# A two-layer attention and spectral-filter kernel: value rows stored by two transfers, block weights loaded behind the first rows' values, twiddle tables laid out by chunk and loaded later

## What is computed

```
# layer 0: 7 x 7 neighbourhood attention, 4 heads of 32 channels, zero padding, then an MLP
xn = layernorm(x); q, k, v = split(xn @ w_qkv + b_qkv)
attn = softmax(q*scale . windows7x7(k) + rpb);  x = x + (attn . windows7x7(v)) @ w_proj + b_proj
x = x + gelu(layernorm(x) @ w_fc1 + b_fc1) @ w_fc2 + b_fc2
# layer 1 on tokens t (4, 3136, 128): q * sum(k * v), then a spectral filter
t = t + q(ln(t)) * sum_tokens(k(ln(t)) * v(ln(t)))
t = t + selected filter bank: irfft(rfft(phi) * rfft(ln(t))) for +/- parts, mixed by M_phi_plus, M_phi_minus,
        plus a 3-tap part with M_u; one of four banks is chosen by log_weights + gumbel
```

## Time and profile before

| | before |
|---|---|
| median of 3 runs | 1872.19 us (1871.04 to 1874.68) |
| the profiled execution, own time | 1875.25 us |
| its span | 1873.9 us |
| PE busy | 1772.8 us, 95% of the span |
| DVE, ACT, POOL busy | 1285.0, 1177.9, 623.3 us |
| mean granted PE clock | 0.976 of full |
| moved by DMA | 183.74 MB, mean 98 GB/s |
| chain that ended last | PE 69%, DVE 11%, DMA 6%, SP's queue 5%, issue 4%, ACT 3%, POOL 1% |

### The profile page before, as it was taken

The page is one execution under the profiler, slowest core; times in us unless marked ns, Lnnn a source line. Parts: engine busy times, 40 slices in busy tenths (PEclk is TensorE's granted clock), DMA queues, the critical chain, the costliest instruction groups (busy, mean ns, idle before and its releaser), DMA issues.

```text
span 1873.9 us, 76356 instructions
## 1 busy us (share of the span) xinstructions
PE 1772.8 (95%) x32475; PEld 1392.8 (74%) x32475; DVE 1285.0 (69%) x3723; ACT 1177.9 (63%) x2555; POOL 623.3 (33%) x799
## 2 busy tenths in 40 slices
PE   5799999999999998999999999999999999999998
PEld 2466676666667666776788888888888888876675
DVE  2477678888867766464477777777777777647665
ACT  4688888878877664433677777777777777640000
POOL 5454555555555543030522123333222233100000
PEclk8799999999999998999999999999999999999999
DMA  3332333343233224398421222122212221367772
GB/s 94 98 90 77 96 95 86 86 108 105 74 91 100 76 70 123 110 240 193 128 63 37 66 67 67 50 63 66 55 37 66 67 67 51 91 181 206 206 205 70
DMA packets 272608, 183.74 MB, mean 98 GB/s; under 512 B 46496, under 2 KB 269630, under 8 KB 270476
## 3 DMA queue, kind: packets, MB, share of 16 engines
q1 hardware_dynamic: 269390, 177.29, 36.2%
q0 software_dynamic: 640, 1.16, 0.2%
q10 hardware_dynamic: 2240, 0.40, 0.1%
HBM read 108.26 MB, written 70.63 MB: 95 GB/s over the span
## 4 chain that ended last, share of the span: by engine, by line
PE 69%; DVE 11%; DMA 6%; SPq 5%; issue 4%; ACT 3%; POOL 1%; DVEq 0%; ACTq 0%; POOLq 0%
PE banks L1363 20%; PE banks L1341 11%; PE banks L1344 9%; PE banks L403 5%; DVE zone L604 3%; PE banks L1180 3%; PE banks L397 3%; PE banks L1551 3%; PE banks L362 2%; PE banks L352 2%; SPq L1479 2%; PE banks L1175 2%; PE banks L376 2%; DMA YL<-Yd 2%; PE banks L410 2%
## 5 line engine op out<-in xcount | busy, mean ns | idle before, releaser
L1396 DVE COPY Gm<-banks 128x448 f32<-128x448 f32 x896 | 553.0, 639 | 218.3 <-PE banks L1341 136.8
L1382 ACT ACTIVATE Gm<-banks 128x448 f32<-128x448 f32 x896 | 515.8, 629 | 192.8 <-PE banks L1341 147.0
L1363 PE MATMUL banks<-Gm,U 128*32 128x128 f32 x12544 | 517.5, 275 | 9.0 <-issue 8.3
L1363 PEld LDWEIGHTS banks<-Gm,U 128*32 128x32 f32 x12544 | 340.1, 110 | 52.3 <-issue 51.2
L1344 PE MATMUL banks<-V,zone 118*32 118x224 bf16 x7040 | 293.0, 259 | 0.7 <-issue 0.6
L1420 POOL COPY U<-UL 128x896 f32<-128x896 f32 (+2 forms) x28 | 49.9, 1782 | 547.4 <-PE banks L1363 441.9
L1341 PE MATMUL banks<-V,zone 118*128 118x224 bf16 x1824 | 215.5, 261 | 0.7 <-ACT qT L1191 0.6
L866 POOL TENSOR_TENSOR W<-W,mx 128x280 f32<-128x280 f32 x196 | 130.2, 664 | 242.6 <-DVE mx L653 241.3
L1344 PEld LDWEIGHTS banks<-V,zone 118*32 118x32 bf16 x7040 | 193.5, 96 | 1.5 <-issue 1.0
L1341 PEld LDWEIGHTS banks<-V,zone 118*128 118x128 bf16 x1824 | 157.2, 98 | 47.9 <-issue 39.8
L1551 PE MATMUL banks<-YC,zone 98*98 98x256 f32 x768 | 174.5, 389 | 3.3 <-DVE YC L1623 3.3
(11 more groups left out here) (164 smaller groups left out, 2546.3 us busy)
## 6 DMA issues: line engine op xcount, KB each, us to landing
Yd<-YS SPq DMA_DIRECT2D x112, 224.0 KB, 4.4
W<-Vd SPq DMA_DIRECT2D x392, 49.0 KB
zone<-Yd SPq DMA_DIRECT2D x32, 392.0 KB
YL<-Yd SPq DMA_DIRECT2D x32, 392.0 KB
UL<-Ud SPq DMA_DIRECT2D x27, 448.0 KB, 4.1
zone<-Mbf SPq DMA_DIRECT2D x28, 256.0 KB
Vd<-W SPq DMA_DIRECT2D x112, 56.0 KB
T<-XR SPq DMA_DIRECT2D x28, 224.0 KB, 3.7
```

The costliest lines, as they stand in the source:

```text
L1363: ins = e.matmul(p[32 * x:32 * x + 32, :], self.U7[(2 * P + ch) % 3][:, sl, 8 * (3 - q):8 * (3 - q) + 32], self.Gm[:, par, r:r + 2, :], st ...
L1382: e.activation(dst, src, ACT.Copy).then_inc(S["gm_act"], 1)
L1396: v.tensor_copy(dst, src).then_inc(S["gm_dve"], 1)
```

## The change

Four edits, in the code of SP's queue and in one table:

1. A row's values go to `Vd` by two transfers in place of four. One takes the even image lines of the row (partitions 0 to 55), one the odd ones, each with the position in the line as its outermost extent (56), then the four parts, then 128 channels. The counts that are waited for on `d_vs0` and `d_vs1` go from 64 to 32 a row.
2. The six weight loads leave `setup(0)` and become `setup(3)`, at unit 11: behind the stores of rows 0 and 1 and before the first tile's load.
3. The twiddle table is laid out by chunk on the host, so that one partition's three rows of a chunk are one run of 336 bytes in place of three of 112.
4. The twiddles of chunks 0 and 1 leave `g_load` and become events `t_load`, at the units of spectrum pieces (6, 5) and (7, 5), the second one ahead of `u_load`.

```diff
@@ order_ab
+        if (w, i) in ((6, 5), (7, 5)):
+            put(u, rests="t_load", n=w - 6)
         if w == 7 and i == 5:
             put(u, rests="u_load")
...
-        order += [("setup", i) for i, at in ((1, 2), (2, 6)) if u == at]
+        order += [("setup", i) for i, at in ((1, 2), (2, 6), (3, 11)) if u == at]
@@ Front.vector
-                    v.wait_ge(S[f"d_vs{n % 2}"], 64 * (n // 2))
+                    v.wait_ge(S[f"d_vs{n % 2}"], 32 * (n // 2))
@@ Front.setup
+        if part == 3:
+            e.dma_start(self.wpr, D["w_proj"]).then_inc(S["d_rest"], 16)
+            e.dma_start(self.wf1, D["w_fc1"]).then_inc(S["d_rest"], 16)
+            e.dma_start(self.wf2, D["w_fc2"].rearrange("(i p) c -> p i c", p=128)).then_inc(S["d_rest"], 16)
+            for i, a in enumerate((D["Wq"], D["Wk"], D["Wv"])):
+                e.dma_start(self.wl1[:, i, :], a).then_inc(S["d_rest"], 16)
...
-        e.dma_start(self.wpr, D["w_proj"]).then_inc(S["d_rest"], 16)
...
@@ Front.sync
-                for m in range(4):
-                    r = 3 + 8 * i + 2 * m
-                    e.dma_start(D["Vd"][b, r:r + 2, 3:59, :], self.VS[n % 2][:, 128 * m:128 * m + 128]).then_inc(S[f"d_vs{n % 2}"], 16)
+                for odd in range(2):
+                    r = 3 + 8 * i + odd
+                    e.dma_start(D["Vd"][b, r:r + 7:2, 3:59, :].rearrange("m w c -> w m c"),
+                                self.VS[n % 2][56 * odd:56 * odd + 56, :].rearrange("w (m c) -> w m c", m=4)
+                                ).then_inc(S[f"d_vs{n % 2}"], 16)
...
-                    e.wait_ge(S["d_vs0"], 64 * ((done + 1) // 2))
-                    e.wait_ge(S["d_vs1"], 64 * (done // 2))
+                    e.wait_ge(S["d_vs0"], 32 * ((done + 1) // 2))
+                    e.wait_ge(S["d_vs1"], 32 * (done // 2))
...
-                for c in range(2):
-                    load_twiddles(e, D, S, c)
+            elif k == "t_load":
+                load_twiddles(e, D, S, n)
@@ load_twiddles
-    return e.dma_start(D["TW"][c % 2][:, :, :], D["c_tw"][:, FC * c:FC * c + FC].rearrange("(o a) s -> o a s", o=1
-                       ).broadcast_to([128, 3, FC])).then_inc(S[f"d_tw{c % 2}"], 16)
+    return e.dma_start(D["TW"][c % 2].rearrange("p a s -> p (a s)"), row_of(D["c_tw"][c].rearrange("a s -> (a s)"))
+                       ).then_inc(S[f"d_tw{c % 2}"], 16)
@@ tables
-    tw = np.stack([tc, ts, tci])
+    tw = np.stack([tc, ts, tci]).reshape(3, NCH, FC).transpose(1, 0, 2)
```

## The result

| | before | after |
|---|---|---|
| median of 20 executions, us | 1876.38 (1869.46 to 1882.09) | 1866.26 (1861.30 to 1875.72) |
| ratio | | 0.9948, 95% interval 0.9934 to 0.9963 |
| profiled execution, us | 1875.25 | 1862.51 |
| its span, us | 1873.9 | 1861.2 |

The change is worth 9.8 us (6.9 to 12.4): faster, as forecast, but by less than the 15.4 us of the forecast. The time, 1866.3, lies 0.8 us above the range. Part of that is the starting point: the three executions at hand had a median of 1872.19, the twenty have 1876.38.

The account below looks back on a forecast made before the run. PE bounds nearly every slice, so time is won only where it stands still or runs at low clock, mostly before 100 us. Gains of 13.4, 1.3 and 0.7 sum to 15.4 us: 1872.2 to 1856.8 us, range 1851.5 to 1865.5.

Parts of the forecast that it names:

- First wait, 6.5 us: At the first `out`: PE no longer waits for window values and runs at 35.5 instead of 42.00, 6.5 us earlier.
- If the weights come after about 32, each us shows on PE: In the front, POOL's first `q_pre` needs the weights; landing near 30 is covered, each us past about 32 delays PE.
- The store's form: SP's value stores, 28 rows: two issues of 0.72 us replace four, freeing 1.4 us of SP per row.
- about 1 us: DMA price of one landed value row (224 KB) with the new stores, between 5.1 us and 0.9 us.
- Stretch up to the tenth `out`: From 35.5 to 71.85 us: at the packing of 60 to 68 us the tenth `out` comes at 58.5, gaining 13.4 us.
- Rival (b): In the front: PE keeps waiting in small pieces at 1.2 GHz, so only 10 us are won, 1862; chance 0.20.
- The later rows gain nothing: Rows after 97.56 us: PE has its own work in full, hiding the 1.4 us of SP freed per row.
- From about 100 us on almost any such gain is kept.: Rest of the program: later steps wait for steps of the order, none for a moment in time, so gains last.
- That wait stays.: PE's 3.95 us before 846.10, for DVE behind `Un` stores ahead of the twiddles in SP's queue, remains.
- Twiddles, 0.7 us: Near 841 us: moving the first two twiddle loads frees SP and removes the 0.66 us wait before 879.47, gaining 0.7 us.
- POOL: In the front: its first `q_pre`, at 28.19 before, may be held 1 to 2 us by the weights, which is covered.
- Rival (e): In the front: SP is caught in the six weight issues, up to 7.43 us each, making it slower, 1893; chance 0.02.

Follow-up runs that it names:

- s1: The kernel before with the new form of the value stores alone, weight loads still ahead of them: 1862.14 us, ratio 0.9924.
- s2: The kernel before with the six weight loads moved behind the first two rows' stores, in the old form of four: 1874.83 us, ratio 0.9992.
- t1: The kernel before with the twiddle table laid out by chunk, its first two loads at their old place: 1878.70 us, ratio 1.0011.
- u2: The kernel before with the last seven rows' `Un` stores issued from ACT's queue in place of SP's: 1877.84 us, ratio 1.0004.
- s3: The kernel before with the twiddle edits alone, layout and place: 1878.37 us, ratio 1.0017.
- s4: The whole change without the twiddle edits, so new stores and moved weights: 1865.05 us, ratio to before 0.9935.
- w4: The kernel before with the store form and the twiddle edits, without the move of the six weight loads: 1865.69 us, ratio 0.9926.
- u1: The whole change with the last seven rows' `Un` stores issued from ACT's queue: 1862.84 us, ratio to before 0.9925.
- u3: Stores and weights of the change without its twiddle edits, and the `Un` stores on ACT's queue: 1863.92 us, ratio to before 0.9929.
- w3: The kernel before with only the fourth stage's filter weights moved behind the load of the first output rows: 1883.75 us, ratio 1.0039.
- x3: The kernel before with only the fourth stage's weights issued in the tail, behind the second pair's spectra: 1882.57 us, ratio 1.0026.
- y3: The kernel before with only the fourth stage's weights moved right behind the third stage's: 1886.39 us, ratio 1.0053.
- w1: The whole change with the fourth stage's filter weights moved behind the load of the first output rows: 1874.04 us, ratio to before 0.9976.
- y1: The whole change with the fourth stage's weights moved right behind the third stage's: 1874.06 us, ratio to before 0.9989.

## Why the prediction was right, and where it failed

- **First wait, 6.5 us.** Right, 42.00 to 35.57. But it was credited to the weights' move together with the store; by s1 the store alone does it (35.02), and by s2 the move alone does not (42.84). "If the weights come after about 32, each us shows on PE" is what s2 shows: they landed at about 38, and PE stood 5.85 us for it.
- **The store's form.** SP's part was right in kind. Issues of 0.72 each were forecast; the four at 19.86 took 0.42 to 1.50, a later pair 0.82 together, the four of s1 0.42 to 0.48 each, and the median over the whole program is 0.41 (0.67 in the old form, of which a row has four). The price of "about 1 us" a landed row is not shown by any run: behind the last issue both rows had landed after 3.6 us in the change and 3.9 in s1 (4.7 before), in company of x rows and weights. That both had landed by about 26.5 was right (26.8). The rule of the Trainium skill ("DMA: Bandwidth & Descriptors", why a DMA increments its semaphore by 16) gives 2 engines for the old form and 14 for the new. The traces agree for the old one: in s2, from 26 to 28 us, with little but old stores under way, the share is 0.14, 2.2 of 16 engines, at 44 GB/s. No row has the new stores by themselves; the change moves 347 GB/s in the same slice, but part of that is weights. The rule of the Trainium skill that two transfers to disjoint halves of the partitions serialize ("DMA: Bandwidth & Descriptors", "Rules for kernel authors") has no cost that shows here; a single transfer was not tried.
- **Stretch up to the tenth `out`.** 13.4 forecast, 13.23 measured; the packing of 60 to 68 us, not the floor, was the right guide. Up to the `out` of 97.56: 14.7 forecast, 14.07 measured. Rival (b) did not come; the clock was 0.82 from 36 to 55 us, where over 0.9 was said: it was at 1.2 GHz from 42 to 46 us, after PE had stood 2.06 and 0.66 us for ACT.
- **The later rows gain nothing.** They gained 1.6 us more, in two steps near 250 and 400 us. But the profiled execution of before was itself slow in its front: t1, u2 and s3, which leave the front as it was, run 1.4 to 1.9 us ahead of it at 400 us. So some 14 to 14.5 of the 15.7 us belong to the change.
- **"From about 100 us on almost any such gain is kept."** This is the step that failed. Six traces have the new store form and the fourth stage's weights in their old place (the change, s1, s4, w4, u1, u3), four the old form and the old front (before, s3, t1, u2). By the means of the two groups the new form is ahead by 14.7 us at 400 and 546 us, 13.2 at 658, 12.6 at 740 and 11.6 at the first product of the tail: some 3 of 15 us are lost (1.2 to 4.2 in each of the six). In the change itself two places show. Near 640 us 1.7 us went back: the same piece of program, in which PE is busy 3.4 of 5 us (650 to 655 before, 634.3 to 639.3 after), is followed by 5 us at a clock of 0.73 in the change and of 1.00 before. Against the trace of before all twelve traces with the new form lose 1.6 or 1.7 us at 576 us, at 658 or at both. Of seven with the old form four do too (u2, w3, x3, y3: 1.4 to 1.6 us) and three do not (s2, s3, t1), so the loss is not the new form's alone. Why the clock fell there stays open; the granted clock is all that the rows show. Near 830 us another 2.0 went: the earlier trace rows's wait grew to 5.95.
- **"That wait stays."** Its cause was read rightly (DVE, behind `Un` stores that land late); its size, 3.95 us, was taken as fixed. It is 4.30, 4.60, 5.76 and 5.95 us in s1, s4, w4 and the change, and 3.53, 3.91 and 4.23 in s3, s2 and t1. That the bytes ahead of the stores set it is shown by w1 to w3, which take 1.9 MB away and have it no more. Why it is longer with the new form stays open. The two kernels of 5.76 and 5.95 are those with the twiddle edits, but s3, which has these edits on the old form, has the shortest wait of all.
- **Twiddles, 0.7 us.** "SP free at 841" was right. The wait of 0.66 is gone in the change, but not for the reason given: it is gone in s1, s4, t1 and u2 too, which leave the twiddle loads where they were, and w4, which moves them, still has 0.32. So the term has nothing to show for it; at the tail's start the change is 11.86 us early, 0.6 less than at 833.
- **POOL.** Its first `q_pre` ran at 29.20 (28.19 before), after 0.87 us for the last weights; covered, as said. Rival (e) did not come: six weight issues took 0.43 to 0.51 us each.
- **The base.** The time missed the forecast by 9.5 us. 4.2 of them come from taking the gain off a median of three that lay that much below the median of twenty; from 1876.4 the same sum gives 1861.0, and the same range, 1855.7 to 1869.7, would have held the result. The other 5.3 are gain that did not come.

The medians leave one thing unsettled. The six kernels with the new store form and no weights moved late lie at 0.9924 to 0.9948, the whole change highest; their mean, 0.9931, is a gain of 12.9 us, closer to the 15.4 of the forecast than the change's 9.8. The intervals overlap, and the parts do not say which of them would cost the 4 us between s1 and the change. It may be none.

## What to carry to other kernels

Look at the outermost extents of a transfer first: one rewritten store was worth the whole change, and the reordering beside it nothing that could be told. Before an order is changed, ask who waits for what moves back: moved alone, the weights freed the tile loads and held POOL and PE instead. A gain early in a long program can be lost in part further on (here some 3 of 15 us), where something other than the sped-up engine bounds; look for slices in which the DMA share is near 1 and PE waits. And where the engines are full for 100 us, moving bytes can move the wait: three places were tried, and each cost more than it freed. Read a merged row of a queue with the durations of its single issues beside it: time in which the queue waits for another engine stands in the same row.

## What the runs showed of the hardware

- An issue can hold its engine for 7.4 us where the DMA engines are full (share 0.87 to 0.91 from 835 to 845 us of the kernel before), whatever the length of its runs: one twiddle load of short runs took 7.43 us, the same load with long runs 7.42 (t1). It is not so for every issue there: a `Un` store at 834.13 took 2.27 us and the next two 0.30.
- Stores with an outermost extent of 2 kept the 16 engines at a share of 0.14 and moved 44 GB/s (s2, 26 to 28 us), and eight of them took SP 10.19 us (before); the same data in four stores of extent 56 took it 1.88 (s1).
- A share near 1 does not mean many bytes: from 845 to 880 us of the change the engines were 0.91 to 1.12 busy in every 5 us, at 138 to 346 GB/s. And a low share does not mean that a transfer lands soon: in y1 the store of `Ud` of 883.50 landed after 19.1 us, though from 895 to 900 the share was 0.29, at 104 GB/s.
- PE can stand for several us and wait for nothing that the profile shows. Gaps named `issue` of 4.53, 6.63 and 9.16 us stood in the three kernels that issue 1.9 MB of weights in the tail; in all others the longest was 3.96. Late instructions would fit; that is not shown.
- The same piece of program was followed by 5 us at a granted clock of 0.73 in one trace and of 1.00 in the other, 16 us later.
